# Layer 1 of a graph kernel: a drain of TensorE behind each lot's last product signals that the lot is summed, in place of the product itself

## The chip, the cores and the metric

The kernel runs on one core of one Trainium2 chip. The metric is the device time of one execution in microseconds (us); lower is better. One change is timed against the kernel before.

## The reference

Two graph layers over 6250 nodes with 512 features and 100,000 edges. The change lies in the second one, layer 1, in its sum over neighbours (`agg` below); the layer also has an attention branch and a batch norm at either end.

```python
h = relu(layernorm(x));  x = x + layer0(h, src, dst)      # graph attention, 8 heads
h = relu(layernorm(x));  x = x + layer1(h, stack([src, dst]))
# layer1:
xn   = batchnorm(h)
msg  = xn[edge_index[0]]                                  # one row of 512 per edge
agg  = segment_sum(msg, edge_index[1], num_segments=N)    # summed per destination node
agg  = agg / max(deg, 1)[:, None]
conv = relu(agg @ W_conv + b_conv)
out  = batchnorm(conv + attention(h) + h)
```

## The kernel before, in words

The edges have been sorted by destination on the chip. They are worked through in chunks of 128 edges. Two chunks make a **lot**, whose destinations all lie in one tile of 128 nodes; four lots (`LR`) make a **row**; there are 440 lots (`LOTS1`) in 110 rows (`ROWS1`). 784 chunks are gathered; a chunk that lies on the border of two tiles serves two lots.

Five engines run side by side in this stage and are held together by counters (semaphores):

- **GpSimd** (`gather_row`, L1133) issues one indirect DMA for each chunk: 128 rows of `h_table`, 2 KB each, into one of 24 places of a ring in `big`. Four chunks are a group; before a group is issued, GpSimd waits on `freed` for its places.
- **ScalarE** (`pass_on`, L1286) sees a group land and adds one to `arrived`. It also writes the next index rows (L531).
- **TensorE** (`sum_row`) goes row by row. It waits for the row's one-hot matrices, makes two bf16 products that count degrees (L1851), reads the places of the four lots from a table into registers (`load_places`, L998 and L1004), and then does the lots. Ahead of every second lot it reads from a table how many groups must have arrived (`load_count`, L1004) and waits on `arrived`. For each lot it waits on `lot1_added` for a free PSUM bank (five banks take turns) and multiplies two one-hot matrices with the two chunks: 128x128 by 128x512 in float32, L1859 (`start`) and L1860 (`stop`). In the trace a float32 product is two MATMUL records with a LDWEIGHTS each. The second product adds one to `lot1_ps` when it is done.
- **VectorE** (`add_row`) waits for that count (L1563) and adds the bank to the node sums in `acc` (L1565), which adds one to `lot1_added`. Behind the first lot of a row it makes the next row's one-hot matrices (L1524).
- **SyncE** waits for certain counts of `lot1_ps` (L1078) and adds one to `freed`, which lets GpSimd gather into places that were read.

Of the kernel before, what the change touches and what calls it, by code (L numbers as in the profile page):

```python
# [16 lines left out]
D = 512  # L17
# [76 lines left out]
def build(nc, x, src, dst, W0, att_w, norm1_g, norm1_b, norm2_g, norm2_b, W_conv, b_conv, Wq, Wk, Wv, Wo, proj, out):  # L94
    with ExitStack() as ctx:
        def sb(name, shape, dt):
            return ctx.enter_context(nc.sbuf_tensor(name, shape, dt))
# [4 lines left out]
        def sem(name):  # L102
            return ctx.enter_context(nc.semaphore(name))

        v, s, g, pet = nc.vector, nc.scalar, nc.gpsimd, nc.tensor
# [17 lines left out]
        onehot = sb("onehot", [P, 2, SB, P], F32)  # L123
# [824 lines left out]
        def lot1_sums(r, b):  # L948
            return (psA[:, 0:D], psA[:, D:2 * D], psC[:, 0:D], psD, psE[:, :])[(r.c * LR + b) % SUMS1]
# [47 lines left out]
        def load_places(engine, r, first):  # L997
            _, at = nc.values_load_multi_w_load_instructions(  # L998
                place_of_lot[:, bass.ds(r, 1), first:first + 4].rearrange("p r b -> p (r b)"), engines=[engine.engine], min_val=0,
                max_val=places[-1], skip_runtime_bounds_check_because="the table holds the places of the ring")  # L1000
            return at

        def load_count(engine, table, r, n, most):
            return engine.value_load(table[:, bass.ds(r, 1), n:n + 1].rearrange("p r u -> p (r u)"), min_val=1, max_val=most)  # L1004
# [4 lines left out]
        lot1_ps = sem("lot1_ps")  # L1009
# [657 lines left out]
        def layer1_tensor(pe):  # L1667
# [57 lines left out]
            for w, ps, name in ((Wq_s, psA, "qT"), (Wk_s, psC, "kT")):  # L1725
                for j in range(KD):
                    for k in range(KD):
                        ins = pet.matmul(ps[:, j * MAXN:(j + 1) * MAXN], w[:, k, j * P:(j + 1) * P], hT[:, k, :],
                                         start=(k == 0), stop=(k == KD - 1))
# [13 lines left out]
            for n in range(2):  # L1743
                for j in range(KD):
                    for t in range(NT):
# [3 lines left out]
                                         start=True, stop=True)  # L1749
# [51 lines left out]
            for h in hs:  # L1801
# [7 lines left out]
                for t in range(NT):  # L1809
                    c = h % 2 * 256 + t * (DH + 1)  # L1810
                    for mt in range(MT):
                        ins = pet.matmul(psE[:, c:c + DH + 1], qfT[:, h % 2, mt, t * P:(t + 1) * P], kvs[:, h, mt, :],
                                         start=(mt == 0), stop=(mt == MT - 1))
# [15 lines left out]
            for t in range(NT):  # L1829
                for k in range(KD):  # L1830
                    ins = pet.matmul(psA[:, t * 512:(t + 1) * 512], attnT[:, k, t * P:(t + 1) * P], Wo_s[:, k, :],
                                     start=(k == 0), stop=(k == KD - 1))
# [15 lines left out]
            def sum_row(r):  # L1848
                pe.wait_ge(onehot1_ready, r(1, 1))
                for u in range(2):  # L1850
                    pet.matmul(row_counts_ps[u], one_column[:, bass.ds(r(1, 0), P)],  # L1851
                               onehot_b[:, r.q, u * LR:(u + 1) * LR, :], start=False, stop=False)
                at = load_places(pe, r(1, 0), 0)
                for b in range(LR):
                    if b % 2 == 0:
                        pe.wait_ge(arrived, load_count(pe, needed_by_quad, r(1, 0), b // 2, 2 * CHUNK_ROWS))
                    pe.wait_ge(lot1_added, r(LR, b + ADD1_CREDIT - SUMS1 + 1))
                    pair = big[:, bass.ds(at[b], 2 * D)]
                    pet.matmul(lot1_sums(r, b), onehot[:, r.q, 2 * b, :], pair[:, 0:D], start=True, stop=False)  # L1859
                    pet.matmul(lot1_sums(r, b), onehot[:, r.q, 2 * b + 1, :], pair[:, D:2 * D],  # L1860
                               start=False, stop=True).then_inc(lot1_ps, 1)
            pe.wait_ge(deg_step, DEG_AT["tile_marks"])
            no_counts(True)
            each_row(pe, ROWS1, CYCLE, sum_row)
            no_counts(False).then_inc(rows_counted, 1)
            pe.wait_ge(deg_step, DEG_AT["row_counts"])
            pe.wait_ge(lot1_added, ADD1_CREDIT + LOTS1)
            for b in range(SB):
                ins = pet.matmul(deg_ps, row_counts[:, b * P:(b + 1) * P], tile_marks[:, b // 2, :], start=(b == 0),
                                 stop=(b == SB - 1))  # L1870
# [660 lines left out]
```

## Time and profile before

| | us |
|---|---|
| median of 3 runs (not profiled) | 3007.24 |
| lowest and highest of them | 3004.78, 3007.37 |
| span of the profiled execution | 3541.0 |
| of it, the stage of the neighbour sums of layer 1 (first gather to last lot) | 2070 to 3260 |
| of it, the gathers of layer 0 | about 440 to 1900 |

The profiled execution's own time is known by its span alone. It is 534 us longer than the median of the runs that were not profiled, so a number of the trace can't be carried over without asking whether it holds without the profiler.

### The profile page before, as it was taken

The numbers are of one execution on the slowest core, as the hardware profiler recorded it, in microseconds if no ns is written. First come the engines' busy times: TensorE is split into PE (matmuls) and PEld (weight loads), VectorE is DVE, ScalarE is ACT, GpSimd is POOL, SyncE is SP. The second block draws the span as 40 slices with busy tenths as digits, with TensorE's granted clock in tenths as the row PEclk, the third lists the DMA queues.
The fourth block names the chain that finished last, engine by engine and source line by source line (L and its number), as shares of the span: only waits on it lengthen the run. The fifth ranks groups of instructions, "written<-read, shape, count | busy, mean of one in ns | idle before, by whom it ended". The sixth has DMA issues, their size and how long they took to land. (4 is left out here: it accounts for less than half of the span.)

```text
span 3541.0 us, 46052 instructions
## 1 busy us (share of the span) xinstructions
PE 2699.5 (76%) x10647; PEld 1671.1 (47%) x10692; DVE 2161.8 (61%) x3783; ACT 995.2 (28%) x3078; POOL 1858.0 (52%) x1883
## 2 busy tenths in 40 slices
PE   6887377777777877777777787877778788788991
PEld 4554256666656656655656652323333333233440
DVE  9999966666666767666668743333333333334668
ACT  6733334444443444434444520000000000000220
POOL 0000255555555556555555446666666666664667
PEclk8998678898988899898898897888889999999995
DMA  5110366666666666666665856666666666565226
GB/s 184 47 40 31 111 180 185 186 189 185 180 182 188 180 191 189 183 192 176 177 189 191 288 152 174 176 180 178 178 176 178 173 173 175 171 174 157 67 66 251
DMA packets 243449, 588.25 MB, mean 166 GB/s; under 512 B 57744, under 2 KB 82832, under 8 KB 243400
## 3 DMA queue, kind: packets, MB, share of 16 engines
q0 software_dynamic: 133120, 443.52, 43.8%
q1 hardware_dynamic: 110280, 144.14, 12.4%
q8 instruction: 23, 0.38, 0.0%
q14 instruction: 26, 0.21, 0.0%
HBM read 533.43 MB, written 54.10 MB: 166 GB/s over the span
## 5 line engine op out<-in xcount | busy, mean ns | idle before, releaser
L506 POOL DMA_INDIRECT big<-feat_table,idx x880 | 841.3, 956 | 1020.8 <-ACT idx L531 407.5
L1133 POOL DMA_INDIRECT big<-h_table,idx x784 | 743.6, 948 | 460.6 <-issue 235.2
L801 PE MATMUL psA<-big,onehot 128*128 128x260 f32 x1760 | 504.0, 436 | 120.1 <-DVE big L683 95.4
L801 PE MATMUL psB<-big,onehot 128*128 128x260 f32 x1760 | 479.8, 420 | 18.6 <-DVE acc L693 13.1
L801 PEld LDWEIGHTS psA<-big,onehot 128*128 128x128 f32 x1760 | 365.4, 216 | 208.3 <-issue 115.2
L557 ACT ACTIVATE big<-big,late_weights 128x65 f32<-128x65 f32 x1760 | 434.4, 343 | 0.0
L801 PEld LDWEIGHTS psB<-big,onehot 128*128 128x128 f32 x1760 | 351.5, 209 | 84.9 <-DVE acc L693 22.2
L531 ACT CAST idx<-minorB 128x8 int32 (+1 forms) x101 | 20.4, 204 | 1142.6 <-DMA big<-h_table,idx 1142.6
L1565 DVE TENSOR_TENSOR acc<-acc,psCD 128x512 f32 x176 | 120.7, 686 | 320.1 <-remote 106.2
L1565 DVE TENSOR_TENSOR acc<-acc,psA 128x512 f32 x176 | 120.7, 686 | 273.6 <-remote 103.3
L1859 PE MATMUL psA<-big,onehot 128*128 x352 | 199.3, 650 | 58.9 <-issue 42.7
L1859 PE MATMUL psCD<-big,onehot 128*128 x352 | 202.0, 658 | 44.1 <-issue 27.4
L683 DVE TENSOR_TENSOR big<-big,psCD 128x1040 f32<-128x1040 f32 x168 | 204.2, 1230 | 1.2 <-issue 1.2
L1860 PE MATMUL psCD<-big,onehot 128*128 x352 | 195.6, 639 | 1.8 <-issue 1.8
L683 DVE TENSOR_TENSOR big<-big,psE 128x1040 f32<-128x1040 f32 x162 | 196.8, 1229 | 0.0
L1860 PE MATMUL psA<-big,onehot 128*128 x352 | 192.9, 631 | 3.6 <-issue 3.6
L693 DVE TENSOR_TENSOR acc<-acc,psB 128x520 f32 x220 | 152.4, 693 | 57.4 <-PE psB L801 29.9
L2445 PE MATMUL psB<-big 128*128 128x512 f32 x392 | 186.1, 620 | 0.0
L693 DVE TENSOR_TENSOR acc<-acc,psA 128x520 f32 x220 | 152.7, 694 | 44.8 <-remote 10.1
L1886 PE MATMUL psA<-big 128*128 128x512 f32 x392 | 179.3, 600 | 0.0
L1851 PE MATMUL psB<-onehot,pad_keys 128*128 128x512 bf16 x176 | 63.7, 425 | 133.9 <-DVE onehot L1524 116.1
L1565 DVE TENSOR_TENSOR acc<-acc,psE 128x512 f32 x88 | 60.4, 686 | 156.0 <-remote 45.1
(447 smaller groups left out, 3960.8 us busy)
## 6 DMA issues: line engine op xcount, KB each, us to landing
nodes_all<-slot_nodes SPq DMA_DIRECT2D x56, 512.0 KB
big<-feat_table,idx POOLq DMA_INDIRECT x880
feat_table<-big SPq DMA_DIRECT2D x49, 264.0 KB, 2.1
x_table<-acc SPq DMA_DIRECT2D x49, 256.0 KB, 3.8
h_table<-big SPq DMA_DIRECT2D x49, 256.0 KB, 4.0
big<-h_table,idx POOLq DMA_INDIRECT x784
big<-h_table SPq DMA_DIRECT2D x49, 256.0 KB, 2.6
big<-x_table SPq DMA_DIRECT2D x49, 256.0 KB, 4.3
```

What stands on the lines that cost most here:

```text
L506: g.indirect_dma_start(ring[:, b.k, q * SB + u, :], None, feat_table, bass.IndirectOffsetOnAxis(ap=idx[:, 2 * b.k + q, u:u + 1], axis=0)). ...
L557: ins = s.activation(part, part, ACT.Copy, scale=late_weights[:, at:at + 1])
L683: v.tensor_tensor(pair, pair, weight_ps[b.k][:, 2 * a * H:(2 * a + 2) * H] .rearrange("p (b h) -> p b h", h=H).unsqueeze(3).broadcast_to([ ...
L693: v.tensor_tensor(d, d, (psA, psB)[a % 2][:, :].rearrange("p (u w) -> p u w", u=2)[:, :, 0:HALF_W], ALU.add).then_inc(lot_added, 1)
L801: ins = pet.matmul(psum[:, 512 * hf:512 * hf + HALF_W], onehot[:, q, u % SB, :], ring[:, b.k, u, HALF_W * hf:HALF_W * (hf + 1)], start=(u ...
L1133: g.indirect_dma_start(big[:, place:place + D], None, h1_table, bass.IndirectOffsetOnAxis(ap=idx[:, r.c % CHUNK_CYCLE, b:b + 1], axis=0)). ...
L1565: v.tensor_tensor(d, d, lot1_sums(r, b), ALU.add).then_inc(lot1_added, 1)
L1851: pet.matmul(row_counts_ps[u], one_column[:, bass.ds(r(1, 0), P)], onehot_b[:, r.q, u * LR:(u + 1) * LR, :], start=False, stop=False)
L1859: pet.matmul(lot1_sums(r, b), onehot[:, r.q, 2 * b, :], pair[:, 0:D], start=True, stop=False)
L1860: pet.matmul(lot1_sums(r, b), onehot[:, r.q, 2 * b + 1, :], pair[:, D:2 * D], start=False, stop=True).then_inc(lot1_ps, 1)
L1886: ins = pet.matmul(psA[:, q * 512:(q + 1) * 512], aggT[:, q, k * P:(k + 1) * P], Wc_s[:, k, :], start=(k == 0), stop=(k == KD - 1))
L2445: pet.matmul(psB[:, q * D:(q + 1) * D], hTbuf[:, q, k * P:(k + 1) * P], W4[:, k, :, :].rearrange("p h o -> p (h o)"), start=(k == 0), stop ...
```

## The change

In `sum_row` the second product of a lot no longer carries the increment of `lot1_ps`. A drain of TensorE stands behind it and carries it. A drain is an instruction of the sequencer: it ends when what the engine was given before is done. There are 440 more instructions on TensorE, one for each lot, and nothing else is altered: `lot1_ps` counts the same lots in the same order.

```diff
                     pet.matmul(lot1_sums(r, b), onehot[:, r.q, 2 * b, :], pair[:, 0:D], start=True, stop=False)
-                    pet.matmul(lot1_sums(r, b), onehot[:, r.q, 2 * b + 1, :], pair[:, D:2 * D],
-                               start=False, stop=True).then_inc(lot1_ps, 1)
+                    pet.matmul(lot1_sums(r, b), onehot[:, r.q, 2 * b + 1, :], pair[:, D:2 * D], start=False, stop=True)
+                    pe.drain().then_inc(lot1_ps, 1)
```

What stands on TensorE from the second lot of a row to the third is this, in both kernels. The listing leaves drains out. Of the names, `psA` and `psCD` are PSUM banks, ISA and REGISTER_ALU are register work and waits of the sequencer, and `tables` holds the counts.

```order
L1860 MATMUL psA<-big,onehot 128x512
L1004 ISA
L1004 TENSOR_LOAD tables
L1004 ISA x2
L1857 REGISTER_ALU
L1859 ISA
L1859 MATMUL psCD<-big,onehot 128x512
```

In the changed kernel a drain stands directly behind the first of these rows (and behind every other L1860 product), so the table read and the register work that follow it are now behind a drain.

## Rows read from the trace of the kernel before

**Rows 1.** The page: span, busy time by engine, TensorE's granted clock in 40 slices.
```profile
span 3541.0 us, 46052 instructions
...
PE 2699.5 (76%) x10647; PEld 1671.1 (47%) x10692; DVE 2161.8 (61%) x3783; ACT 995.2 (28%) x3078; POOL 1858.0 (52%) x1883
...
PEclk8998678898988899898898897888889999999995
```

**Rows 2.** Busy time, granted clock, DMA share by stretch: layer 1's sums, then short stretches.
```profile
2070.00:3260.00 1190.00, 928.71 (x1966) 375.01 (x2010) 431.79 (x574) 23.83 (x103) 743.76 (x785) 0.90 0.61 174
...
2624.00:2627.00 3.00, 2.70 (x3) 1.17 (x4) 0.59 (x1) 0.00 (x0) 2.39 (x3) 0.50 0.71 187
...
2664.00:2672.00 8.00, 6.71 (x16) 2.88 (x17) 4.79 (x7) 0.00 (x0) 6.17 (x7) 1.00 0.70 196
```

**Rows 3.** Who waited for whom, GpSimd: total us, times, longest.
```profile
POOL big L1133 <- issue: 235.2, 721, 3.1
...
POOL big L1133 <- SPq L1078: 189.4, 62, 4.9
...
POOL big L506 <- PE psA L801: 151.0, 85, 7.3
POOL big L506 <- PE psB L801: 119.5, 68, 2.9
POOL big L506 <- remote: 111.2, 48, 2.8
```

**Rows 4.** Gathers in order of time: start, us; then all of L1133.
```profile
2604.48 0.95 POOL L1133 DMA_INDIRECT big<-h_table,idx  x1 [0.30 <-issue]
2605.74 0.95 POOL L1133 DMA_INDIRECT big<-h_table,idx  x1 [0.30 <-issue]
...
L1133 POOL DMA_INDIRECT big<-h_table,idx x784: 943/949/1153, 2070.4 to 3237.6; - x196
```

**Rows 5.** TensorE in order of time, one whole row of lots without a wait.
```profile
3236.72 0.61 PE L1851 MATMUL psB<-onehot,pad_keys 128*128 128x512 bf16 x2
3237.18 1.02 PE L1859 MATMUL psCD<-big,onehot 128*128 x2
3238.03 1.02 PE L1860 MATMUL psCD<-big,onehot 128*128 x2
3238.89 1.02 PE L1859 MATMUL psE<-big,onehot 128*128 x2
...
3244.04 0.61 PE L1851 MATMUL psB<-onehot,pad_keys 128*128 128x512 bf16 x2
```

**Rows 6.** All engines in order of time, a row that starts with TensorE empty.
```profile
2664.09 0.62 PE L1851 MATMUL psB<-onehot,pad_keys 128*128 128x512 bf16 x2 [0.17 <-DVE onehot L1524]
...
2665.91 1.12 PE L1859 MATMUL psE<-big,onehot 128*128 x2 [1.20 <-DVE acc L1565]
...
2667.30 0.19 PEld L1859 LDWEIGHTS psA<-big,onehot 128*128 128x128 f32 x1 [0.24 <-issue]
2667.73 1.02 PE L1859 MATMUL psA<-big,onehot 128*128 x2
```

**Rows 7.** By line, that row, last all rows: ns min/median/max, first and last start.
```profile
L1857 PEldq ALU_OP  x1: 32/32/32, 2665.7 to 2665.7; - x1
...
L1004 PEldq FUSED_REGOPS  x2: 46/98/151, 2666.4 to 2666.9; - x2
...
L1857 PEldq ALU_OP  x1: 32/32/32, 2667.2 to 2667.2; - x1
...
L1563 DVEq EVENT_SEMAPHORE  x1: 21/21/21, 2667.9 to 2667.9; - x1
...
L1849 PEldq ALU_OP  x97: 2/32/718, 2106.5 to 3238.9; - x97
```

**Rows 8.** The kernel's end, where TensorE has a drain already.
```profile
L95 PEldq DRAIN  x1: 2127/2127/2127, 3467.2 to 3467.2; - x1
...
3466.06 3.25 PE L1910 MATMUL psB<-big,maxd 128*128 128x512 f32 x4 [3.49 <-DVE big L1634]
3467.23 0.50 PEld L1910 LDWEIGHTS psB<-big,maxd 128*128 128x128 f32 x2 [0.88 <-DVE big L1634]
```

**Rows 9.** TensorE and VectorE in order of time, where a count comes late.
```profile
2612.57 1.02 PE L1860 MATMUL psE<-big,onehot 128*128 x2
...
2617.72 1.02 PE L1860 MATMUL psCD<-big,onehot 128*128 x2
2622.47 0.62 PE L1851 MATMUL psB<-onehot,pad_keys 128*128 128x512 bf16 x2 [3.73 <-DVE onehot L1524]
...
2620.51 0.69 DVE L1565 TENSOR_TENSOR acc<-acc,psE 128x512 f32 x1 [8.19 <-remote]
2621.12 1.22 DVE L1524 TENSOR_TENSOR onehot<-psCD,nodeB 128x1024 f32<-128x1024 f32 x1
```

## The prediction

> **What bounds the kernel now.** The page comes first [rows 1]: TensorE is busy for 76% of the span, more than any other engine, and GpSimd for 52%. Neither share says what ends last in the stage that is changed. There [rows 2], in the 1190 us from 2070 to 3260, TensorE is busy for 928.7 us and GpSimd for 743.8 us, and both wait now and then.
>
> Next I look at who holds GpSimd up [rows 3] and at its gathers [rows 4]. A gather takes 0.95 us and the next starts 0.30 us behind it, so the pitch is 1.25 us. 784 gathers at that pitch are 980 us, which no other engine's work can shorten. The real stretch of the gathers is longer mainly by one wait: 189.4 us for SyncE's release of places (L1078), which follows TensorE's count of lots.
>
> What does TensorE need for its own work? Where it does not wait [rows 5], a product starts 0.86 us after the one before (3237.18, 3238.03, 3238.89), a lot takes 1.72 us, and a whole row of four lots with its two bf16 products takes 3244.04 - 3236.72 = 7.32 us. That is 110 x 7.32 = 805 us. So TensorE has about 175 us of slack against the gathers, 1.6 us in a row.
>
> **Which time does this trace stand for?** The span is 3541.0 us [rows 1] and the runs without a profiler have 3007.24: 533.8 us less. Take away GpSimd's waits for released places in both layers, 189.4 in layer 1 and 151.0 + 119.5 + 111.2 = 381.7 in layer 0 [rows 3]: 571.1 us in all, which gives 2970. Nearly the whole difference is thus the size of those waits. Many of them have one origin, which shows in one place [rows 9]. The lot in `psE` has its last product from 2612.57 to 2613.59, yet VectorE adds it only at 2620.51, after 8.19 us for which no releaser shows. TensorE goes on to 2618.3, then stands still, since VectorE makes the next one-hot matrices too. My reading is that the profiler delays counts that ride on products, and that a run without it is paced by the gathers in both layers: for layer 1 some 980 us, 10 us for the last chunks, and 12 us of waits that may remain (the share 189/571 of the 37 us by which 3007 exceeds 2970), 1002 us in all.
>
> **The change part by part.**
>
> *What it removes.* An increment on 440 products. With the products in a stream at 0.86 us each [rows 5], none of them shows a cost, so I count 0.
>
> *What a drain does.* There is one at the end of the program [rows 8]. It starts at 3467.23 and takes 2.127 us, to 3469.36. The last product on TensorE ends at 3466.06 + 3.25 = 3469.31. So it held the sequencer until the array was done and ended 0.05 us later. Behind each lot, therefore, the sequencer stops until the lot is complete, and all it did ahead of time comes after that. Four prices follow, for a row in which the sequencer never gets ahead. Such a row starts at 2664.09 [rows 6].
>
> 1. *From a lot's start to its count.* L1859 starts at 2665.91, the last pass of the lot at 2667.30 (the next lot's weights are loaded beside it), and VectorE sees the count at 2667.9 [rows 7]: 2.0 us. With a few hundredths for the drain's own end: 2.02. Four lots are 8.08 us.
> 2. *From a drain to the next lot.* The register step L1857 is at 2665.7 and the product at 2665.91 [rows 6, 7]: 0.2 us, and 0.05 from the drain to that step. Three times in a row: 0.75 us.
> 3. *The table read ahead of the third lot.* Its register work starts at 2666.4 and the wait on `arrived` is at 2667.2 [rows 7]: 0.8 us. It lay under the first lot's products. Behind a drain nothing covers it.
> 4. *The row's start.* From the bf16 products to the first lot are 2665.91 - 2664.09 = 1.82 us [rows 6], of which the products are under half a microsecond. The rest is the table reads, which are hidden in a stream (3237.18 - 3236.72 = 0.46 us [rows 5]). With two register steps ahead, 0.1 us each: 2.02 us.
>
> The sum is 8.08 + 0.75 + 0.8 + 2.02 = 11.65 us in place of 7.32: 4.3 us more in a row, over twice the slack of 1.6. TensorE becomes the bound of the stage: 110 x 11.65 = 1282 us, and it begins about 12 us after the first gather, as GpSimd starts at 2070.4 while TensorE is busy with earlier work to about 2082. The stage takes 1294 us where it took 1002: +292 us. I take off 6 us for rounding in the short steps. **3007 + 286 = 3293 us.**
>
> *What else moves.* Behind the drain on TensorE are queued the wait on `arrived`, the wait on `lot1_added` and the one-hot wait. VectorE's own work is 4 x 0.69 + 1.22 = 4.0 us in a row (0.69 us an add, and 1.22 us for the matrices of a row [rows 9]), so it does not pace. GpSimd fills the ring and waits for releases. Nothing outside the stage is touched.
>
> *Bounds.* From below: if the drain costs only the lot's completion beyond its stream, 2.02 - 1.72 = 0.3 us four times, the row is 8.5 us, still under the 8.9 of the gathers, and the time stays at 3007. From above: a register step of 32 ns can take 718 ns [rows 7]. One of these in each row adds 77 us, two 154 us. I take the middle sum, since each of its terms has a row in which the sequencer was not ahead, and keep both ends. Against a bound by the traced stage itself (1190 us, late counts included) the gain in time would be 1294 - 1190 = 104 us, or 3111.
>
> **The clock.** After the pause of 3.73 us the granted clock is 0.50, the lower level of 1.2 GHz, from 2624 to 2627. In the row that starts at 2664.09 with a pause of 1.20 us before its first lot it stays at 1.00, 2.4 GHz [rows 2, 6, 9]. The changed row's pauses are at most about 1.4 us, so I keep the upper level. If instead the clock stayed at the lower level, the 7.3 us of streaming in a row would double: 110 x 7.3 = 803 us more, and some 4100 us.
>
> The Trainium skill's page "TensorE: Matmul & The Clock Gate", section "A second HAM failure mode: psum-queue depth-cycling", speaks against this change: short idles between groups of products, with PSUM banks taking turns, made the clock swing between its two levels. By it the time would lie between the two sums above. The trace here agrees only for long pauses.
>
> **The rivals.**
>
> - *The drain is hidden.* TensorE's slack of 1.6 us in a row swallows it: 3007, no change. For it speaks that TensorE does wait for gathers. Against it speaks the drain of 2.127 us [rows 8], with the table reads that then stand open. It decides if a row stays under 8.9 us. Chance 0.07.
> - *The late counts also exist without the profiler.* Then the stage before is 1190 us and the change costs 104 us: 3111. For it speaks that nothing in the trace names the profiler as their cause. Against it speaks the sum of 571 us against 534. Chance 0.10.
> - *Faster.* The counts are late in every run, a drain's count is not, and the drain does not keep the sequencer from working ahead. Then GpSimd's 189.4 us of waits go [rows 3]: 2818. It decides where a row of TensorE stays under the gathers' 8.9 us while counts come on time. Two things must hold that the rows speak against. Chance 0.04.
> - *The clock falls.* Up to 4100, and 3500 if it falls for a fourth of the time. Chance 0.05.
>
> **How the numbers follow.** The forecast has 0.74; its own range goes from 3180 (steps that run faster without the profiler: 1 us less in each row) to 3400 (one long register step in most rows, and rounding). The range takes in the second rival and so reaches from 3095 to 3410; outside are the hidden drain, the gain, and most of the clock's case, under 0.2. Faster by over 0.2%: 0.04. Within 0.2%, about what a measurement of this kernel can tell from no change: 0.07. Slower by over 0.2%: 0.89.
>
> **What would show it.** In the new trace there are 440 drains on TensorE's sequencer. Rows in which it waits for nothing should take 11 to 12 us in place of 7.32; L1859's pauses should be about 0.5 us beyond the stream inside a pair, 1.3 us ahead of the third lot and 1.4 us at a row's start. GpSimd's wait for L1078 should grow from 189 to about 300 us, ACT's wait on `arrived` should no longer pace anything, and the granted clock should be near 1.00. The prediction is wrong if the pitch of a row stays near 9 us, if drains are short while products still run, or if the clock is at the lower level in rows without a long pause.

## The result, and the profile after

The changed kernel takes 3345.23 us (median of 3 runs, 3345.09 to 3347.39) where the kernel before takes 3007.24. The ratio is 1.1135, with a 95% interval of 1.1120 to 1.1151: 338 us slower. The forecast was 3293 us with a range of 3095 to 3410, and slower with a chance of 0.89.

The page of the changed kernel first, against [rows 1]: span, busy time by engine, TensorE's granted clock, the chain that ended last by engine and by line, and the group of layer 1's gathers.

```profile
span 3343.3 us, 46492 instructions
...
PE 2610.6 (78%) x10647; PEld 1519.7 (45%) x10692; DVE 2167.8 (65%) x3783; ACT 993.2 (30%) x3078; POOL 1853.3 (55%) x1883
...
PEclk8998779999999999998899999999999999999995
...
issue 18%; PEldq 14%; PE 9%; PEld 6%; DVE 3%; DMA 1%; POOL 1%; ACT 0%; SPq 0%; DVEq 0%; POOLq 0%; ACTq 0%
PEldq L1861 8%; PE psA L1886 5%; PEldq L1004 3%; PEldq L998 2%; PEld psA L1859 1%; PEld psCD L1859 1%; DVE acc L1565 1%; POOL big L1167 1%; DMA h_table<-big 1%; PEld psA L1860 1%; PEld psCD L1860 1%; PE psB L1674 1%; PEld psE L1859 1%; PE psCD L1878 1%; PEldq L1859 1%
...
L1133 POOL DMA_INDIRECT big<-h_table,idx x784 | 741.0, 945 | 585.8 <-SPq L1078 308.5
```

There are 440 instructions more, the drains. TensorE's sequencer (PEldq) now holds 14% of the chain that ended last: the drains at L1861, and the table reads at L1004 and L998 that came into the open. GpSimd waits 308.5 us for released places; about 300 were forecast, though as a growth from 189, and the second trace of the kernel before (experiment 1) has 22.2. The span now agrees with the times of the runs, 3343.3 and 3345.2, which that of [rows 1] did not. The first experiment takes that up.

One row of lots in the changed kernel, TensorE alone in order of time, the counterpart of [rows 5]:

```profile
2500.46 1.12 PE L1859 MATMUL psCD<-big,onehot 128*128 x2 [1.21 <-issue]
2501.42 1.02 PE L1860 MATMUL psCD<-big,onehot 128*128 x2
2502.79 1.12 PE L1859 MATMUL psCD<-big,onehot 128*128 x2 [0.34 <-issue]
2503.74 1.02 PE L1860 MATMUL psCD<-big,onehot 128*128 x2
2505.84 1.12 PE L1859 MATMUL psE<-big,onehot 128*128 x2 [1.07 <-DVE acc L1565]
2506.80 1.02 PE L1860 MATMUL psE<-big,onehot 128*128 x2
2508.16 1.12 PE L1859 MATMUL psA<-big,onehot 128*128 x2 [0.34 <-issue]
2509.12 1.02 PE L1860 MATMUL psA<-big,onehot 128*128 x2
2510.45 0.62 PE L1851 MATMUL psB<-onehot,pad_keys 128*128 128x512 bf16 x2 [0.31 <-issue]
2512.32 1.12 PE L1859 MATMUL psA<-big,onehot 128*128 x2 [1.24 <-issue]
```

The row takes 2512.32 - 2500.46 = 11.86 us. From lot to lot it is 2.33, 3.05, 2.32 and 4.16 us, where a stream has 1.72 each and 2.18 over the row's end. The products still follow each other inside a lot as in a stream. The releaser named for the third lot, VectorE's add, is merely the last to speak: the next listing has the register reads that fill this pause, and experiment 7 takes them out of it. It gives the first drain and register work behind drains by line, with the count, ns min/median/max, and first and last start, in the stretches from 2500.5 to 2502, to 2503, and from 2504 to 2506.

```profile
L1861 PEldq DRAIN  x1: 1855/1855/1855, 2500.6 to 2500.6; - x1
...
L1857 PEldq ALU_OP  x1: 32/32/32, 2502.6 to 2502.6; - x1
...
L1004 PEldq FUSED_REGOPS  x2: 46/98/151, 2504.9 to 2505.4; - x2
L1004 PEldq TENSOR_LOAD <-tables x1: 313/313/313, 2505.0 to 2505.0; - x1
L1004 PEldq SEQ_ASSERT  x1: 18/18/18, 2505.6 to 2505.6; - x1
```

The drain starts 0.15 us behind the lot's start, as soon as the sequencer has handed the products over, and holds it for 1.855 us. Then comes everything that it used to do ahead. The median of all 440 drains is 1.855 us too.

The stage as a whole in the changed kernel: busy time by engine, granted clock, DMA share and GB/s, against [rows 2].

```profile
1733.00:3060.00 1327.00, 953.15 (x1966) 319.39 (x2010) 438.67 (x574) 23.18 (x102) 740.98 (x784) 0.99 0.54 156
```

The granted clock is 0.99 on the whole, but not everywhere. Eight times in the stage it stands at 0.50, the lower level, for about one lot. The first is at 1758 us, where the kernel before has one too (experiment 1's trace, at 1759 us); the other seven are new. Each of the seven is at the first lot of a row behind a turn of the loop over rows, which comes every ten rows (L991) and puts about 0.3 us more between the last drain and the bf16 products. One of them: the loop's branch by line, then TensorE in order of time, then the stretch of the slow lot.

```profile
L991 PEldq COMPARE_BRANCH  x1: 208/208/208, 1984.2 to 1984.2; - x1
...
1986.54 2.04 PE L1859 MATMUL psA<-big,onehot 128*128 x2 [1.21 <-issue]
1988.37 1.84 PE L1860 MATMUL psA<-big,onehot 128*128 x2
1990.52 1.12 PE L1859 MATMUL psA<-big,onehot 128*128 x2 [0.31 <-issue]
...
1986.40:1990.30 3.90, 3.67 (x4) 1.14 (x4) 0.00 (x0) 0.00 (x0) 0.88 (x1) 0.56 0.54 162
```

That lot takes 1990.52 - 1986.54 = 3.98 us where the same step is 2.33 in the row above. The pauses of 0.3 to 1.3 us left the clock at the upper level nearly everywhere, and cost it at seven of the ten turns of the loop.

### The profile page after: what moved, and what is told of

The parts are those of the page before. It is cut to its first block, busy times and chain, and to the rows that moved or that the text cites. A ratio compares the mean times of both kernels' runs of the same rounds, so it can differ in the third digit from the quotient of the medians.

```text
span 3343.3 us, 46492 instructions
## 1 busy us (share of the span) xinstructions
PE 2610.6 (78%) x10647; PEld 1519.7 (45%) x10692; DVE 2167.8 (65%) x3783; ACT 993.2 (30%) x3078; POOL 1853.3 (55%) x1883
## 4 chain that ended last, share of the span: by engine, by line
issue 18%; PEldq 14%; PE 9%; PEld 6%; DVE 3%; DMA 1%; POOL 1%; ACT 0%; SPq 0%; DVEq 0%; POOLq 0%; ACTq 0%
PEldq L1861 8%; PE psA L1886 5%; PEldq L1004 3%; PEldq L998 2%; PEld psA L1859 1%; PEld psCD L1859 1%; DVE acc L1565 1%; POOL big L1167 1%; DMA h_table<-big 1%; PEld psA L1860 1%; PEld psCD L1860 1%; PE psB L1674 1%; PEld psE L1859 1%; PE psCD L1878 1%; PEldq L1859 1%
## 5 line engine op out<-in xcount | busy, mean ns | idle before, releaser
L1133 POOL DMA_INDIRECT big<-h_table,idx x784 | 741.0, 945 | 585.8 <-SPq L1078 308.5
L801 PE MATMUL psA<-big,onehot 128*128 128x260 f32 x1760 | 442.3, 395 | 15.9 <-DVE big L683 13.8
L801 PE MATMUL psB<-big,onehot 128*128 128x260 f32 x1760 | 433.7, 389 | 7.2
L801 PEld LDWEIGHTS psA<-big,onehot 128*128 128x128 f32 x1760 | 319.0, 191 | 101.1 <-issue 37.0
L801 PEld LDWEIGHTS psB<-big,onehot 128*128 128x128 f32 x1760 | 317.3, 190 | 64.1 <-DVE acc L693 17.5
L1859 PE MATMUL psA<-big,onehot 128*128 x352 | 202.4, 658 | 128.5 <-issue 81.0
L1859 PE MATMUL psCD<-big,onehot 128*128 x352 | 197.2, 642 | 130.3 <-issue 81.7
L1860 PE MATMUL psA<-big,onehot 128*128 x352 | 185.7, 610 | 0.0
L1860 PE MATMUL psCD<-big,onehot 128*128 x352 | 179.8, 592 | 0.0
L1859 PEld LDWEIGHTS psA<-big,onehot 128*128 128x128 f32 x352 | 53.2, 190 | 264.6 <-issue 264.4
L1859 PEld LDWEIGHTS psCD<-big,onehot 128*128 128x128 f32 x352 | 52.3, 188 | 261.3 <-issue 261.3
```

Of the source, the lines that this page charges most:

```text
L801: ins = pet.matmul(psum[:, 512 * hf:512 * hf + HALF_W], onehot[:, q, u % SB, :], ring[:, b.k, u, HALF_W * hf:HALF_W * (hf + 1)], start=(u ...
L1133: g.indirect_dma_start(big[:, place:place + D], None, h1_table, bass.IndirectOffsetOnAxis(ap=idx[:, r.c % CHUNK_CYCLE, b:b + 1], axis=0)). ...
```

## The experiments

**1. The kernel before once more.** No edit. It was to show which of its times the first trace stands for.

> The kernel before, profiled and timed once more. Theory A (the traced span of 3541.0 us was one execution whose product counts came late, and the runs without a profiler were not like it): a time of 3007, and a new trace either near 3007 us with no waits of several us for counts, and gathers of layer 1 that stand some 980 us from the first to the last, or long again if the profiler always does it. Rival (a rate of TensorE's counts that belongs to this code): 3007 again, and the trace again 3541 with the same 189 us of waits of GpSimd for L1078.

Measured: 3003.58 us, ratio 0.9999 (0.9990 to 1.0009). The new trace has a span of 3004.2 us. GpSimd's waits in layer 1, all gathers by line, and the stage, of this second trace of the kernel before:

```profile
POOL big L1133 <- issue: 216.3, 710, 0.3
...
POOL big L1133 <- SPq L1078: 22.2, 73, 0.3
...
L1133 POOL DMA_INDIRECT big<-h_table,idx x784: 942/946/1151, 1734.1 to 2713.2; - x196
...
1734.00:2722.00 988.00, 855.59 (x2010) 350.04 (x2010) 428.38 (x573) 22.84 (x103) 741.57 (x784) 1.00 0.73 209
```

The 784 gathers stand 979 us from the first start to the last, a pitch of 1.25 us. The wait for released places is never longer than 0.3 us, which is the usual step between two gathers. So the stage was paced by the gathers and took 988 us; the 189.4 us of [rows 3] and the late count of [rows 9] belonged to that one execution. The profiler as such did not make them either, since this execution had a profiler too. What did is open. The first trace also holds only 21,755 records of semaphore updates, about half of the 42,897 of the second; whether the two belong together no run shows.

**2. A drain that carries no count.** The product keeps its increment.

```diff
                     pet.matmul(lot1_sums(r, b), onehot[:, r.q, 2 * b + 1, :], pair[:, D:2 * D],
                                start=False, stop=True).then_inc(lot1_ps, 1)
+                    pe.drain()
```

> Nothing but a drain behind each lot; the second product keeps its count. Theory A (the cost is that the drain stops the sequencer, so that the register reads and weight loads behind it are in the open): 3345, as with the changed kernel. Rival (the cost is that the count rides on a sequencer's instruction and so comes later to VectorE and SyncE): 3007.

Measured: 3330.85 us, ratio 1.1094 (1.1075 to 1.1112). So 327 of the 338 us come with a drain alone, against 3003.7 of the kernel before on the same chip. The way in which the count travels is worth the other 11 to 14 us, about 0.03 us for each lot: from lot to lot inside a pair it is 2504.73 - 2502.45 = 2.28 us here; with the count on the drain it is 2.29 in most rows and 2.33 in the row shown above. TensorE in order of time:

```profile
2502.45 1.12 PE L1859 MATMUL psA<-big,onehot 128*128 x2 [1.24 <-issue]
2503.41 1.02 PE L1860 MATMUL psA<-big,onehot 128*128 x2
2504.73 1.12 PE L1859 MATMUL psCD<-big,onehot 128*128 x2 [0.30 <-issue]
```

**3 and 4. Half of the drains, in two places.** Both have 220 drains and the products keep their counts. In the first they stand behind lots 0 and 2 of a row (`b % 2 == 0`), in the second behind lots 1 and 3 (`b % 2 == 1`).

```diff
                                start=False, stop=True).then_inc(lot1_ps, 1)
+                    if b % 2 == 0:
+                        pe.drain()
```

> 220 drains, behind lots 0 and 2 of each row, where only one register step and a weight load stand behind the drain; the products keep their counts. Theory A: a row of TensorE is 7.32 + 2 x 0.60 = 8.52 us (in the changed kernel a lot that follows so takes 2.32 us in place of 1.72), still under the 8.9 us of the gathers: 3007 to 3020. Rival B (each drain has one price, 338 / 440 = 0.77 us): 3176.

> 220 drains again, but behind lots 1 and 3 of each row, where a table read stands behind the drain; the products keep their counts. Theory A: a row of TensorE is 7.32 + 1.33 (lot 1 to lot 2 takes 3.05 us in the changed kernel) + 1.97 (lot 3 to the next row's first lot takes 4.15 us there and 2.18 in a stream) = 10.62 us, 1.7 us over the gathers: 110 x 1.67 + 12 = 196 us more, 3203. Rival B (each drain has one price): 3176, the same as with the drains inside the pairs.

Measured: inside the pairs 3015.5 us, ratio 1.0042 (1.0027 to 1.0056); between the pairs 3208.0 us, ratio 1.0684 (1.0666 to 1.0702). The same number of the same instruction costs 12 us in one place and 204 in the other, so one price for each drain does not explain it. TensorE with the drains inside the pairs, one whole row:

```profile
2500.28 0.61 PE L1851 MATMUL psB<-onehot,pad_keys 128*128 128x512 bf16 x2
2500.73 1.05 PE L1859 MATMUL psCD<-big,onehot 128*128 x2
...
2502.94 1.12 PE L1859 MATMUL psCD<-big,onehot 128*128 x2 [0.30 <-issue]
...
2504.75 1.02 PE L1859 MATMUL psE<-big,onehot 128*128 x2
...
2508.75 0.61 PE L1851 MATMUL psB<-onehot,pad_keys 128*128 128x512 bf16 x2
```

This row takes 8.47 us, 8.52 was worked out, and the gathers need 8.9. The table reads still run ahead, under the lots without a drain. With the drains inside and then between the pairs, GpSimd waits for released places for:

```profile
POOL big L1133 <- SPq L1078: 18.0, 59, 0.3
...
POOL big L1133 <- SPq L1078: 201.8, 113, 4.7
```

Part of the contrast is the slack of 1.6 us in a row: on TensorE itself the two placings add 1.15 and about 3.3 us to a row, and the gathers cover the first of them.

The 12 us with the drains inside the pairs lie at the stage's end. GpSimd waits for the last add from the end of its last gather, once 8.3 us in the second trace of the kernel before, and 19.7 us here:

```profile
POOL onehot L1145 <- DVE acc L1565: 8.3, 1, 8.3
...
POOL onehot L1145 <- DVE acc L1565: 19.7, 1, 19.7
```

**5. One drain in a row of lots.** As before, with `if b == LR - 1`.

> 110 drains, one behind the last lot of each row; the products keep their counts. Theory A: a row of TensorE is 7.32 + 1.97 = 9.29 us against 8.9 of the gathers: 110 x 0.37 + 12 = 53 us more than 3004, 3057. Rival (a drain has one price of 0.77 us): 3089.

Measured: 3070.94 us, ratio 1.0223 (1.0206 to 1.0240), 67 us more than the kernel before where 53 were worked out and 85 by one price. It lies between the two, 14 us above the one and 18 below the other, so this time alone does not decide between them. The rows do: most take 9.29 us, as worked out. GpSimd waits 62.5 us for L1078, so the gathers have just ceased to be the bound. Of the 14 us beyond the sum, 6 lie at the stage's end, where GpSimd's last wait is 26.6 us against 8.3, 18 more where 12 were allowed. The other 8 lie among the rows, where the rows at a turn of the loop take longer, and six lots run at the lower clock.

**6. A wait in place of the drain.** TensorE waits for the lot's own count, which the product carries.

```diff
                                start=False, stop=True).then_inc(lot1_ps, 1)
+                    pe.wait_ge(lot1_ps, r(LR, b + 1 + LOT1_CREDIT))
```

> No drain: behind each lot TensorE waits until lot1_ps shows the lot's own count, which the product carries. Theory A (what costs is that the sequencer stops until the lot is done, whatever stops it): within 20 us of the 3331 us of the run with drains that carry no count. Rival (the drain instruction itself flushes or restarts something): clearly less, near 3004 plus a register step of 0.1 us for each lot, 3050 at most.

Measured: 3282.19 us, ratio 1.0931 (1.0913 to 1.0949). Both numbers were missed: it is 279 us slower than the kernel before, far more than the rival's 50, but 49 us, or 0.11 us for each lot, faster than with a drain that carries no count. TensorE in order of time:

```profile
2502.10 1.12 PE L1859 MATMUL psA<-big,onehot 128*128 x2 [1.00 <-DVE acc L1565]
2503.05 1.02 PE L1860 MATMUL psA<-big,onehot 128*128 x2
2504.22 1.12 PE L1859 MATMUL psCD<-big,onehot 128*128 x2
```

From lot to lot inside a pair it is 2.12 us in place of 2.28. Where the register steps stand shows why. By line, for the lot that starts at 2502.10: the wait's own step, that of L1857, and those of L1859.

```profile
L1862 PEldq ALU_OP  x1: 32/32/32, 2502.3 to 2502.3; - x1
...
L1857 PEldq EVENT_SEMAPHORE  x1: 51/51/51, 2502.4 to 2502.4; - x1
...
L1859 PEldq FUSED_REGOPS  x2: 42/42/42, 2502.0 to 2504.1; - x2
```

The wait's step and that of L1857 are done while the products run, and only the step of L1859, at 2504.1, comes behind the last product (2503.05 + 1.02 = 2504.07). Behind a drain, L1857's step comes after it too, 0.09 us before that of L1859, and the drain's own end takes the rest of the 0.16 us. Where a table read stands behind the lot, the wait is cheaper by 0.06 us only; two steps of each kind make 0.44 us in a row, or the 49 us. So four fifths of the cost (279 of 338 us) are that the sequencer stops until the lot is complete. Some 48 us come with the drain in place of a wait, with no count on it, and the last 11 to 14 us with the count that rides on it.

**7. The changed kernel with the table read ahead of the drain.** `load_count` for the third lot is issued behind the second lot's products and ahead of its drain.

```diff
+                need = load_count(pe, needed_by_quad, r(1, 0), 0, 2 * CHUNK_ROWS)
                 for b in range(LR):
                     if b % 2 == 0:
-                        pe.wait_ge(arrived, load_count(pe, needed_by_quad, r(1, 0), b // 2, 2 * CHUNK_ROWS))
+                        pe.wait_ge(arrived, need)
...
+                    if b == 1:
+                        need = load_count(pe, needed_by_quad, r(1, 0), 1, 2 * CHUNK_ROWS)
                     pe.drain().then_inc(lot1_ps, 1)
```

> The changed kernel, with the table read for the third lot issued ahead of the second lot's drain, under its products. Theory A: lot 1 to lot 2 takes 2.32 us in place of 3.05, so a row loses 0.73 us: 110 x 0.73 = 80 us less than 3345, 3265. Rival (the pause ahead of the third lot is the wait on arrived, not the read): 3345.

Measured: 3255.89 us, ratio 1.0839 (1.0821 to 1.0857), 89 us less than the changed kernel where 80 were worked out. It was the read that lay open, not the wait on `arrived` behind it, nor VectorE's add, which the profile of the changed kernel named there: both are still in place.

**8. All register reads under products.** In addition the last lot's drain of a row moves behind the next row's bf16 products and table reads (one count is taken off at the start for the first row's drain, and one drain stands behind the loop).

```diff
                 need = load_count(pe, needed_by_quad, r(1, 0), 0, 2 * CHUNK_ROWS)
+                pe.drain().then_inc(lot1_ps, 1)
                 for b in range(LR):
...
-                    pe.drain().then_inc(lot1_ps, 1)
+                    if b < LR - 1:
+                        pe.drain().then_inc(lot1_ps, 1)
```

> As the kernel with the read ahead, and the last lot's drain of a row stands behind the next row's bf16 products and table reads, so that all register reads lie under products. Theory A: three lots of 2.32 us, and from the fourth to the next row's first 1.72 + 0.46 + 0.60 = 2.78 us: 9.74 in place of 11.85 us in a row, 232 us less than 3345, 3113. Rival (the drains themselves make most of the cost): above 3200.

Measured: 3092.93 us, ratio 1.0296 (1.0279 to 1.0313). With the same 440 drains and one more behind the loop, 252 of the 338 us are gone; 232 were worked out. First this kernel's drains between rows by line, then TensorE in order of time, then the stage from its third row on:

```profile
L1855 PEldq DRAIN  x110: 13/448/2297, 1742.2 to 2799.0; - x110
...
2500.82 1.12 PE L1861 MATMUL psCD<-big,onehot 128*128 x2 [0.31 <-issue]
...
2503.12 1.12 PE L1861 MATMUL psCD<-big,onehot 128*128 x2 [0.31 <-issue]
...
2507.70 1.12 PE L1861 MATMUL psA<-big,onehot 128*128 x2 [0.31 <-issue]
...
2510.44 1.12 PE L1861 MATMUL psA<-big,onehot 128*128 x2 [0.31 <-issue]
...
1765.00:2812.00 1047.00, 903.75 (x1915) 315.16 (x1958) 421.96 (x546) 20.43 (x97) 717.46 (x760) 1.00 0.66 191
```

The drains between rows are short, 0.448 us in the median, since most of the lot's time went by under the table reads. From the last lot's start to the next row's first it is 2.74 us where it was 4.16, and the row takes 9.62 us, still over the gathers' 8.9. The pauses between rows are now about as short as those inside a row, and the clock has no stretch at the lower level from the third row to the last; some 11 of the 252 us are that. It remains slower than the kernel before.

## Why the prediction was right, point by point

**The bound.** It was read that the gathers pace the stage at a pitch of 1.25 us, with about 1.6 us of slack for TensorE in a row. The second trace shows it, and the two placings of 220 drains show the slack: an added 1.15 us in a row is covered, an added 3.3 us is not.

**Which time the first trace stands for.** The step that took GpSimd's waits off the span gave a stage of 980 + 10 + 12 us. The second trace has 988. The step was right in kind. The reason that I gave, a delay that the profiler causes, fell: another profiled execution of the same kernel has no late counts. The remainder of 12 us was not there. In the reading of [rows 9] the last product before the pause ends at 2618.74 and not at 2618.3, on which nothing rests.

**The drain.** "It held the sequencer until the array was done" is what the runs show: 1.855 us of drain behind most lots, at most 3.520 (a lot at the lower clock).

**The four prices** of a row, forecast and measured from start to start of a lot: inside a pair 2.27 and 2.33, ahead of the third lot 3.07 and 3.05, over the row's end 4.04 and 4.16. The row came to 11.86 us in place of 11.65. Most rows of the stage take 11.82 us, and the mean is 11.96. The signs came as named: beyond a stream it is 0.61 us inside a pair, 1.33 ahead of the third lot and 1.41 at a row's start (about 0.5, 1.3 and 1.4 were named). The term that was too small is the step from a drain to the next lot: the first register step follows the drain by 0.10 to 0.13 us and not by 0.05, and at the row's start, where the price has two register steps of 0.1 us, this step was left out.

**The sum.** 286 us were forecast and 338 measured. Of the 52 us missing, 110 x 0.21 = 23 us are the row; 14 us are the remainder in the stage before (1002 worked out, 988 measured); 6 us I had taken off for rounding. The other 10 are what the measured stage has beyond its rows, 1327 - 12 - 110 x 11.86 = 10 us, and the trace has them: the seven lots at the lower clock make their rows 1.4 to 1.7 us longer, 11 us in all, and ten turns of the loop at 0.3 us are 3, less 4 us because most rows take 11.82.

**The rivals.** The hidden drain does occur, but only for the drains inside pairs. The late counts don't exist in ordinary runs, so 3111 had no ground.

**The clock.** The prediction kept the upper level because pauses were at most about 1.4 us. That held for the stage as a whole (0.99), but not at seven turns of the loop, where the longest pause is still about 1.3 us. A lower clock in rows without a long pause was named as a sign of being wrong; it was there, in seven rows of 110, worth 11 us. So the choice of level was right by size, while the reason for it was too simple. The Trainium skill's page "TensorE: Matmul & The Clock Gate", section "A second HAM failure mode: psum-queue depth-cycling", has short idles that make the clock swing. The trace agrees in kind and not in size: the time of 3345 us lies between the two sums that the prediction gave for it, but 11 us of it are the clock's. That the turn of the loop brings the fall is argued from where the falls lie; the last experiment, whose pauses are short throughout, has none of them.

## What to carry to other kernels

An instruction that stops a sequencer until its engine is done costs what the sequencer used to do ahead, so look at what stands behind it before asking what it costs itself. Ahead of a register step 220 drains added 1.15 us to a row of TensorE, which its slack of 1.6 us covered, and 12 us to the time; ahead of table reads the same 220 added about 3.3 us to a row and 204 us to the time. Where such a stop can't be avoided, put register reads, table reads and the next independent products ahead of it. And when a profiled span is far from the unprofiled times, work out which waits make up the difference, and profile again before trusting a stage's bound.

## What the runs showed of the hardware that I had not expected

An execution of the kernel before, profiled, took 3541 us with counts of finished products that reached the other engines late: by about 7 us in [rows 9], and by 20 us at the worst. There the lot's last product and the add that waited for it are these:

```profile
2119.11 1.02 PE L1860 MATMUL psCD<-big,onehot 128*128 x2
...
2140.12 0.69 DVE L1565 TENSOR_TENSOR acc<-acc,psCD 128x512 f32 x1 [14.12 <-remote]
```

The same kernel profiled again took 3004 us and has none of it, nor has any of the eight other traces. A wait on a semaphore is cheaper for TensorE's sequencer than a drain that carries no count by 0.11 us a lot on the mean, though both stop it for the same lot. The granted clock can fall to its lower level for a single lot with no pause of TensorE longer than about 1.3 us ahead of it: it did so at seven of ten turns of the loop in the changed kernel.
